# Fusion matmuls of a depthwise-separable stage over 128 rows, with zeroed rows behind row 96

## What is computed

```python
# layer 0: two state-space blocks over 4096 tokens, a pooled branch, a 1x1 fusion, batch norm, + x
x = L0(x)
# layer 1: three depthwise convolutions (3x3, 5x5, 7x7), joined, and a 1x1 convolution over 288 channels
h = group_norm(x)
combined = concatenate([dw3(h), dw5(h), dw7(h)], axis=1)
x = x + einsum('bihw,oi->bohw', combined, wf[:, :, 0, 0]) + bf
# layers 2 and 3: attention without softmax and a quantised MLP over the 4096 tokens of each image
t = tokens(x)
for layer in (2, 3):
    t = t + attention(layernorm(t)) @ Wff + bff
    t = t + ffn_fp8(layernorm(t))
out = images(t)
```

## Time and profile before

| | |
|---|---|
| median of three runs | 4113.82 us |
| profiled execution, its own time | 4110.38 us |
| its span in the trace | 4108.6 us |
| TensorE busy | 3482.1 us (85% of the span) |
| VectorE busy | 3421.2 us (83%) |
| GpSimd busy | 2847.0 us (69%) |
| ScalarE busy | 2397.9 us (58%) |
| mean granted TensorE clock | 0.931 |
| token block | from 3392.8 us to the end |

### The profile page before, as it was taken

The page is one execution under the profiler, slowest core; times in us unless marked ns, Lnnn a source line. Parts: engine busy times, 40 slices in busy tenths (PEclk is TensorE's granted clock), DMA queues, the critical chain, the costliest instruction groups (busy, mean ns, idle before and its releaser), DMA issues. The chain is left out here.

```text
span 4108.6 us, 38662 instructions
## 1 busy us (share of the span) xinstructions
PE 3482.1 (85%) x10080; PEld 1402.5 (34%) x10080; DVE 3421.2 (83%) x4323; ACT 2397.9 (58%) x4121; POOL 2847.0 (69%) x2332
## 2 busy tenths in 40 slices
PE   6899999999999999999999999999860887675765
PEld 2333333333333333333333333333320334453553
DVE  3999999999999999999999999999984004778686
ACT  5666776666666677666666677666632221435445
POOL 3988889999999888999999988899870000213123
PEclk8999999999999999999999999999985999786767
DMA  2555555555556555555545555555458877100001
GB/s 85 166 157 169 163 163 159 164 168 156 160 163 176 164 162 157 156 164 157 156 154 166 162 157 163 151 158 163 145 150 207 240 236 187 47 16 12 20 1 31
DMA packets 296513, 588.62 MB, mean 143 GB/s; under 512 B 82743, under 2 KB 151994, under 8 KB 295142
## 3 DMA queue, kind: packets, MB, share of 16 engines
q1 hardware_dynamic: 229222, 516.93, 42.7%
q10 hardware_dynamic: 67072, 69.23, 6.5%
HBM read 532.16 MB, written 58.28 MB: 144 GB/s over the span
## 5 line engine op out<-in xcount | busy, mean ns | idle before, releaser
L796 POOL TENSOR_TENSOR prod<-states,c_rows 128x512 f32<-128x512 f32 x1536 | 1919.9, 1269 | 183.3 <-DVE states L726 149.2
L726 DVE TENSOR_TENSOR_SCAN states<-decay,carry,bpsum 128x512 f32<-128x512 f32 x1344 | 1676.9, 1259 | 0.0
L455 PE MATMUL ypsum<-prod,identity 128*128 128x512 f32 x3072 | 1596.4, 603 | 0.5 <-POOL prod L796 0.3
L561 ACT ACTIVATE decay<-delta,decay_rate 128x512 f32<-128x512 f32 x1344 | 934.8, 711 | 314.0 <-DVE states L726 309.4
L706 DVE TENSOR_TENSOR bpsum<-bpsum,dx 128x512 f32<-128x512 f32 x1344 | 904.6, 673 | 138.6 <-PE bpsum L448 124.4
L455 PEld LDWEIGHTS ypsum<-prod,identity 128*128 128x128 f32 x3072 | 584.2, 194 | 422.7 <-issue 280.8
L448 PE MATMUL bpsum<-b_rows,select 96*128 96x512 bf16 x1344 | 522.8, 389 | 209.4 <-DVE states L726 206.7
L448 PEld LDWEIGHTS bpsum<-b_rows,select 96*128 96x128 bf16 x1344 | 129.5, 96 | 972.6 <-DVE states L726 689.1
L1662 POOL TENSOR_TENSOR y<-y,b 128x384 f16<-128x384 f16 x64 | 68.3, 1067 | 544.8 <-ACT y L1466 544.8
L561 ACT ACTIVATE bpsum<-delta,decay_rate 128x512 f32<-128x512 f32 x192 | 132.6, 691 | 309.5 <-DVE states L726 308.6
L495 PE MATMUL mm<-h_norm,w_xs 96*128 96x512 f32 x512 | 262.8, 599 | 6.0 <-ACT h_norm L627 6.0
(11 more groups left out here) (194 smaller groups left out, 4555.9 us busy)
## 6 DMA issues: line engine op xcount, KB each, us to landing
c_rows<-bc_map SPq DMA_DIRECT2D x512, 512.0 KB, 3.8
c_rows<-bc_map SPq DMA_DIRECT2D x512, 256.0 KB, 4.0
b_wide<-bc_map ACTq DMA_DIRECT2D x128, 256.0 KB, 4.5
image<-normed_map SPq DMA_DIRECT2D x192, 96.1 KB
depthwise_map<-dw_sums ACTq DMA_DIRECT2D x96, 192.0 KB, 4.3
dw_parts<-depthwise_map SPq DMA_DIRECT2D x16, 1152.0 KB, 14.1
b_wide<-bc_map ACTq DMA_DIRECT2D x128, 128.0 KB, 4.2
normed_map<-padded SPq DMA_DIRECT2D x8, 1155.0 KB, 11.7
```

The costliest lines, as they stand in the source:

```text
L455: pe.matmul(ypsum[:, group % Y_BANKS, :], identity[:, :], prod[:, n % P_RING, :], start=s == 0, stop=s == STATES - 1).then_inc(summed, 1)
L561: act.activation(into, delta[k % 2][:, g, :], ACT.Exp, scale=decay_rate[:, ORDER[k][0], g, s:s + 1]).then_inc(done, 1)
L726: dve.tensor_tensor_scan(states[:, n % H_RING, :], by, add, carry[:, at, u:u + 1], ALU.mult, ALU.add).then_inc(scanned, 1)
L796: pool.tensor_tensor(prod[:, n % P_RING, :], states[:, n % H_RING, :], c_rows[:, n // C_STATES % C_RING, n % C_STATES, :], ALU.mult).then_ ...
```

## The change

`wf` and `parts` are declared with 128 partitions in place of 96. The loads and the small bias matmul in the first block name rows 0 to 95 of them explicitly, as before. The fuse matmuls (line 1295) keep their text, and since they take whole tiles they now read 128 rows of both. GpSimd clears rows 96 to 127 of both at the head of the token block, ahead of its four memsets, and the three waits for `rest_zero` go from 4 to 6.

```diff
-        wf = sb("wf", [C, 3, C])
+        wf = sb("wf", [128, 3, C])
-            rest = [(ident[:, :], dram["identity"]), (wf[:, :, :], dram["wf_t"]),
+            rest = [(ident[:, :], dram["identity"]), (wf[0:C, :, :], dram["wf_t"]),
-        last = pe.matmul(mp[0:C, 0, 0:1], wf[:, k, :], vecs[:, col:col + 1], start=k == 0, stop=k == 2)
+        last = pe.matmul(mp[0:C, 0, 0:1], wf[0:C, k, :], vecs[:, col:col + 1], start=k == 0, stop=k == 2)
-        parts = sb("dw_parts", [C, G_RING, 2, ROW_BLOCKS, 3, ROW_BLOCKS * HALF_SIDE])
+        parts = sb("dw_parts", [128, G_RING, 2, ROW_BLOCKS, 3, ROW_BLOCKS * HALF_SIDE])
-                    sp.dma_start(parts[:, i % G_RING, :, :, :, :].rearrange("c o j k n -> c o (j k n)"),
+                    sp.dma_start(parts[0:C, i % G_RING, :, :, :, :].rearrange("c o j k n -> c o (j k n)"),
-                pe.wait_ge(rest_zero, 4)
+                pe.wait_ge(rest_zero, 6)
-                act.wait_ge(rest_zero, 4)
+                act.wait_ge(rest_zero, 6)
-                dve.wait_ge(rest_zero, 4)
+                dve.wait_ge(rest_zero, 6)
             def _(pool):
+                pool.memset(wf[C:, :, :], 0.0).then_inc(rest_zero, 1)
+                pool.memset(parts[C:, :, :, :, :, :].rearrange("p g o j k n -> p (g o j k n)"), 0.0).then_inc(rest_zero, 1)
                 pool.memset(h_t[C:, :], 0.0).then_inc(rest_zero, 1)
                 pool.memset(h8[C:, :], 0.0).then_inc(rest_zero, 1)
                 pool.memset(w1[C:, :, :], 0.0).then_inc(rest_zero, 1)
```

## The result

The changed kernel takes 4118.4 us, the median of 16 runs, against 4110.89 us for the kernel before on as many. The ratio is 1.0019, with a 95% interval from 1.0011 to 1.0027, which is 4.5 to 11.1 us. One of the changed kernel's 16 runs took 6004.79 us at a granted clock of 0.549, where the others lie between 4115.04 and 4122.24 us at 0.93; the ratio leaves it out, and the median of the other 15 is 4118.1 us. The interval shows the change to be slower, by less than the 0.3% that the prediction took as the bound of "same". The forecast was 4122 us, within 4113 to 4130, with "same" as the likeliest reading.

The account below looks back on a forecast made before the run. The token block's head was taken as bound by the first fuse's start, then TensorE's own pace. Delay +9.9 us, 128-row matmuls 0 and clock 0, on a base of 4111.6, gave 4121.5, rounded to 4122 us; range 4113 to 4130.

Parts of the forecast that it names:

- The start of the first fuse: Head of token block: GpSimd's fourth memset ends at 3400.84 us, the first load lands at 3401.46; 0.62 us of cover.
- The memsets: GpSimd at the token block's head: clearing `wf` takes 0.34 us and `parts` 10.34, adding 10.56 us to its queue.
- The delay at the head: Token block's head: TensorE's first fuse waits for the later memsets, 10.56 less 0.62 us of cover, +9.9 us.
- The rest of the way: From first fuse to end: no load becomes late, nothing is paid back; 707 us as now, within 3 us.
- The matmuls over 128 rows at full clock: Fuse matmuls: 128 rows keep 0.43 us a record and 5.15 us a fuse, a term of 0.
- The clock: Slow parts of the fuses: more rows don't raise the granted clock; 0 taken, between -7.8 and 0.
- rival 1: Fuses: 128 rows give back clock, up to 7.8 us against the head's +9.9, about 4114 us; chance 0.13.
- 3 us of scatter: Slow starts after pauses: their length varies from run to run, counted as plus or minus 3 us with centre 0.
- The total: Whole kernel: 4122 us, 0.20% slower against the median, with "same" the likeliest reading at 0.65.
- Rival 2: Sixteen fuses: 32 changes between 96 and 128 rows each uncover a weight load, 9.0 us, 4130.5 in all; chance 0.10.
- rival 3: Token block's head: memsets hidden by a later load or faster clearing, delay 0 to 5 us, about 4114; chance 0.05.

Follow-up runs that it names:

- The control: Kernel before, 96 rows, with its wait for the four old memsets moved behind the first eight fuses; 4113.04 us, ratio 1.0000.
- 96-row partner: Changed kernel with both memsets and the waits for six kept, but fuse matmuls over rows 0 to 95 only; 4121.35 us, ratio 1.0025 in the last series.
- two clears with 96 rows: Changed kernel with the memset of `parts` done twice and fuse matmuls over 96 rows; 4134.80 us, ratio 1.0057, and 4134.22 us, 1.0057.
- two or four clears: Changed kernel, 128 rows, with the memset of `parts` done twice (4128.57 us, ratio 1.0041; 4129.32 us, 1.0044) or four times (4149.89 us, 1.0094).

## Why the prediction was right, and where it wasn't

**The start of the first fuse** was read as two releases, GpSimd's last memset and, 0.62 us later, the load. The control confirms that the load was the later one: nothing was gained by taking the memsets out of the way.

**The memsets.** 0.34 and 10.34 us were forecast from 0.833 ns an element and 0.10 us fixed; they took 0.33 and 10.33. The slope held at twice the longest length in the trace of before.

**The delay at the head.** +9.9 us forecast, 9.88 in the profile of the changed kernel, and again 9.87 and 9.88 in its repeats. This was the term that decided. Its surest part is the end of the memsets; less sure is how much the load had hidden. The load took 8.25 us in the profile of before and 8.72, 8.80 and 8.81 in the three others in which it held the first fuse, so against such an execution the delay would be about 0.5 us smaller. The 9.88 us have the same profile of before as their base as the forecast has, so they test the memsets and not the load.

**The rest of the way.** That no later wait takes the delay back holds: 706.0, 707.3 and 706.9 us with the change, 707.0 before. One reading was off by a group: load 4 is issued when group 0 has been added up (the wait is for a count of 1), not group 1. Nothing hangs on it, since either moves with the fuses.

**The matmuls over 128 rows at full clock.** 0 forecast, 0 found: the beat stays at 0.43 us and a fuse at 5.15 us.

**The clock.** The step that was too strong is "Rows don't order the clock in this trace. I take 0". For the changed kernel it stands as far as the runs can tell: against its 96-row partner on one chip it was 1.3 us slower, within intervals of some 4 us to either side, and with the delay taken away the two differed by 0.8 us the other way. But the reason given for it, two rises of 5.9 us with 96 and with 128 rows, was one of each. With a longer pause ahead the slow part with 128 rows lasted 3.2 and 4.0 us and with 96 rows 5.9 and 6.65 us, and the totals differed by 5 to 6 us. So rival 1 may have named something real, at less than half its 7.8 us. Against the delay of 20.3 us the 128-row kernel gets back 2.1 and 3.7 us, and the 96-row kernel comes out 2.6 and 2.8 us above it. In the changed kernel no such gain was told from noise, so it could not have turned the result. The 3 us of scatter that were counted for the slow starts were about right; the same kernel's profiles differed by 1.3 us behind the first fuse, two clears with 96 rows by 2.8.

**The total.** The forecast of 4122 is 3.6 us above the median. The 9.9 us were put on a base of 4111.6; 16 runs of before have 4110.89, so 0.7 us of it is the base, and 0.5 us was rounded up. The rest, 2.4 us (9.9 against the measured 7.5), is inside the interval of the ratio, whose upper end is 11.1 us, and the series on one chip gave 11.5 for the same kernel. Rival 2 (changes of tile size) is excluded at its 9 us by the run with 128 rows and no delay, and rival 3 (hidden memsets) by the first fuse's start, 18.6 us in each of five profiles with one clear.

**What stays open.** Whether the number of rows shortens the rise after a long pause, and by what means. Three profiles with 128 rows and two or four clears against two with 96 rows and two clears are the evidence, and repeats of one kernel differ by up to 0.7 us in the first two fuses. Of the 5 to 6 us between the totals the first fuses show 1.1 to 1.8. About 1 us more lies in slow parts that take either length in the same kernel, and the profile of 710.3 us is 2.8 us longer than its repeat. The rest of the difference between the medians isn't explained.

## What to carry to other kernels

When a change asks for zeroed memory, price the clear by elements on its engine and look at who stands on its semaphore: 12288 elements cost GpSimd 10.3 us, and three engines waited for all of it although the first fuse read a quarter. One semaphore count per slot, in order of use, took the same clears off the path. Going from 96 to 128 rows left the pace of these matmuls at 0.43 us a record, so what the padding cost here was the time to fill the pad.

And where the idle row names an engine that ended 0.7 us before, look for the other release in the chain: here it was a load, and it set how much of the clear was covered.

## What the runs showed that had not been expected

With the first fuse held back 20 us or more, fuses over 128 rows ran at the lower level of the clock for 3.2 to 4.0 us (first two fuses 11.94 to 12.28 us), and those over 96 rows for 5.9 and 6.65 us (13.35 and 13.69 us). After the shorter pauses of before and of the change both took 12.87 to 13.79 us. The Trainium skill (TensorE: Matmul & The Clock Gate, Part 1: The HAM clock gate) says that the number of slow matmuls after a pause varies between runs of one kernel. The three profiles of the changed kernel agree, with 12.87, 13.15 and 13.58 us. That page ties the clock to how busy the engine was. The six profiles with 96 rows stay within 0.5 us and the long-pause profiles with 128 rows lie 1.0 us or more below all of them, so chance alone is an unlikely reading; three profiles don't settle it.
